# A graph-network layer on one core: a second tile of source columns in every fourth pair, built by VectorE, with narrower one-hots

## The reference, cut to what matters

```python
msg_in = jnp.concatenate([nodes[row], nodes[col], edge_features], axis=-1)
messages = relu(msg_in @ mW1 + mb1) @ mW2 + mb2
aggregated = jax.ops.segment_sum(messages, col, num_segments=nodes.shape[0])
upd_in = jnp.concatenate([nodes, aggregated], axis=-1)
x = _layernorm(x + relu(upd_in @ uW1 + ub1) @ uW2 + ub2)
```

## Time and profile before

| | us |
|---|---|
| median of 3 runs | 1884.84 (1877.70 to 1885.05) |
| the profiled execution | 1882.74 |
| its span, on which every time in the rows lies | 1880.9 |

### The profile page before, as it was taken

One profiled execution on the slowest core, in us unless ns is written; L12 is line 12 of the kernel. 1 busy time (PEld: TensorE's weight loads), 2 busy tenths in 40 slices (PEclk: granted clock), 3 DMA queues, 4 the chain that ended last, 5 costly groups with the idle time before them and its releaser, 6 DMA issues.

```text
span 1880.9 us, 44708 instructions
## 1 busy us (share of the span) xinstructions
PE 1466.1 (78%) x8940; PEld 1317.6 (70%) x8940; DVE 1374.8 (73%) x8194; ACT 1452.3 (77%) x12577; POOL 1383.9 (74%) x1478
## 2 busy tenths in 40 slices
PE   6777667787977778778977688777878887968778
PEld 6766667777766767667776677666767776867676
DVE  5746777787777777777777678778777777777773
ACT  4147878787888888888888878788787887887974
POOL 5677777777777777777777777777777777777772
PEclk9887778777787887887688877888786878787876
DMA  8555445544544544544544444454454454455441
GB/s 235 169 126 121 119 106 127 124 115 116 126 113 116 126 111 118 126 115 114 126 119 118 118 122 121 112 126 122 107 126 117 112 126 122 107 125 121 114 114 29
DMA packets 99674, 226.91 MB, mean 121 GB/s; under 512 B 45451, under 2 KB 61656, under 8 KB 86782
## 3 DMA queue, kind: packets, MB, share of 16 engines
q1 hardware_dynamic: 42532, 124.03, 26.3%
q0 software_dynamic: 46816, 94.40, 21.1%
q10 hardware_dynamic: 10046, 5.59, 1.2%
HBM read 214.24 MB, written 9.60 MB: 119 GB/s over the span
## 4 chain that ended last, share of the span: by engine, by line
POOL 71%; issue 23%; PE 3%; DMA 2%; DVE 1%; DVEq 0%; POOLq 0%; ACT 0%
POOL gath L798 68%; POOL hid L782 1%; DMA hid<-in_x_dram,idx_all 1%; DMA gath<-table_src,idx_all 1%; POOL raw_x L782 1%; PE ps_sum L934 1%; PE ps_pre L914 0%; DVEq L504 0%; DVE col_x L543 0%; DVE lhs L1275 0%; DVE hid L1304 0%; PE ps_pre L921 0%; PE ps_node L987 0%; PE ps_pre L981 0%; PE ps_pre L987 0%
## 5 line engine op out<-in xcount | busy, mean ns | idle before, releaser
L798 POOL DMA_INDIRECT gath<-table_src,idx_all x1415 | 1335.5, 944 | 431.2 <-issue 429.4
L520 ACT COPY col_x<-xz 64x1 f32 x11840 | 1137.3, 188 | 59.3 <-issue 55.0
L914 PE MATMUL ps_pre<-rhs,lhs 128*128 128x128 f32 x3226 | 576.2, 352 | 382.7 <-DVE lhs L1275 379.4
L914 PEld LDWEIGHTS ps_pre<-rhs,lhs 128*128 128x128 f32 x3226 | 536.9, 260 | 404.1 <-DVE lhs L1275 400.7
L543 DVE TENSOR_TENSOR col_x<-xz 64x2 int32 x6698 | 525.6, 148 | 135.9 <-issue 128.5
L934 PE MATMUL ps_sum<-onehot,hid 128*128 128x96 f32 x3322 | 471.9, 303 | 4.1 <-ACT rhs L1067 4.1
L934 PEld LDWEIGHTS ps_sum<-onehot,hid 128*128 128x128 f32 x3322 | 451.2, 218 | 25.6 <-issue 23.2
L1304 DVE TENSOR_TENSOR hid<-ps_pre,gath 128x1024 f32<-128x1024 f32 x202 | 246.7, 1221 | 288.1 <-DMA gath<-table_src,idx_all 269.8
L1105 ACT ACTIVATE hid<-hid 128x1024 f32<-128x1024 f32 x202 | 211.7, 1048 | 102.8 <-DVE hid L1304 99.0
L1275 DVE TENSOR_SCALAR_CACHE_REDUCE lhs<-lhs,place 96x1024 f32<-96x1024 int32 x208 | 262.1, 1260 | 15.7 <-DMA lhs<-in_dst_dram 15.7
L1268 DVE TENSOR_TENSOR onehot<-ps_iota,dst_rel 128x768 f32<-128x768 f32 (+1 forms) x209 | 196.7, 942 | 0.1
(11 more groups left out here) (136 smaller groups left out, 686.5 us busy)
## 6 DMA issues: line engine op xcount, KB each, us to landing
lhs<-in_dst_dram SPq DMA_DIRECT2D x99, 768.0 KB
lhs<-in_edgeT_dram SPq DMA_DIRECT2D x98, 256.0 KB
gath<-table_src,idx_all POOLq DMA_INDIRECT x1415
table_src<-gath SPq DMA_DIRECT2D x12, 512.0 KB, 7.5
xwin<-in_xT_dram SPq DMA_DIRECT2D x208, 24.0 KB
lhs<-in_dst_dram SPq DMA_DIRECT2D x10, 384.0 KB, 4.3
out_dram<-late_b ACTq DMA_DIRECT2D x48, 64.0 KB, 2.2
xz<-in_xT_dram ACTq DMA_DIRECT2D x4, 512.0 KB, 11.6
```

Of the source, the lines that this page charges most:

```text
L520: ins = copy(col_x[:, k, start + n + j:start + n + j + 1], col)
L798: pool.indirect_dma_start(gath[0:m, k, j * H:(j + 1) * H], None, table_src, src_by_tile(p, j, m)).then_inc(gathered[k], 16)
L914: mm = nc.tensor.matmul(to[0:m, j * H:(j + 1) * H], lhs[:, k, j * P:j * P + m], rhs[:, k, :], start=True, stop=not by_cols)
```

## The change

**In each fourth pair, a second tile by copied columns.** `EX_FIRST` is 15. For p = 15, 19, ..., 203 (48 pairs) the tile before the last, `EX_TILE`, is not gathered either. Its 128 columns are copied into the new tensor `col_e` (two buffers), all by DVE. The work is spread over four steps: in each step the function `extra` loads 16 registers and issues 8 two-column instructions, once in the middle of the step and once at its end. PE adds one matmul for the tile (L962 of the changed file).

**Early registers.** The two register loads of the first `col_x` batch move from behind the one-hots to ahead of `add_gathered`.

**Columns.** ACT copies 56 and DVE 72 (40 and 32), where they were 60 and 68.

**Narrow one-hots.** The first four tiles of a pair write only columns 0 to 47 of the window, the last four 20 to 75. The rest is zeroed once ahead of the loop (three memsets). The sums that DVE adds are 76 wide, not 96. PE's matmuls keep their width of 96. The check of the input is stricter to match: for the input here the destinations reach at most 33 nodes from the window's start in a pair's first half, and 27 to 65 in its second, so the same path is taken.

**Raw gathers.** POOL no longer waits between raw pairs.

```diff
-COL_ACT = 60
-COL_LOADS = (12, 16, 12, 12, 8)
+COL_ACT = 56
+COL_LOADS = (12, 16, 12, 8, 8)
 COL_DVE = 32
+EX_FIRST = 15
+EX_TILE = PT - 2
+EX_STEPS = 4
+EX_PART = P // EX_STEPS
...
+        def extra_of(p):
+            q = p + 2 + (EX_FIRST - p - 2) % SLOTS
+            return (q, EX_STEPS - (q - p - 1)) if has_extra(q) else None
...
-            return rows_of(p) if is_last(p) else PT - has_cols(p)
+            return rows_of(p) if is_last(p) else PT - has_cols(p) - has_extra(p)
...
             for r in range(RAW):
-                if r > 0:
-                    pool.wait_ge(raw_got[r - 1], 16 * PT)
...
+                    if extra:
+                        pe.wait_ge(cols_ext, ext_count(p))
+                        mm = nc.tensor.matmul(to[:, j * H:(j + 1) * H], col_e[:, p // SLOTS % 2, :], w_src[0:D, :], start=False, stop=True)
...
-                for first, t, m in parts(p):
-                    to = onehot[0:m, k, first * WIN:(first + t) * WIN].rearrange("p (t w) -> p t w", t=t)
+                for first, t, m, lo, hi in window_parts(p):
+                    to = onehot[0:m, k, first * WIN:(first + t) * WIN].rearrange("p (t w) -> p t w", t=t)[:, :, lo:hi]
...
+            def extra(p, half):
+                q, part = extra_of(p) or (None, None)
+                if q is not None:
+                    if q == EX_FIRST and part == 0 and half == 0:
+                        dve.wait_ge(cols_tabled, 8)
+                    start = part * EX_PART + half * EX_PART // 2
+                    held = load_regs(dve, q // SLOTS, start, EX_PART // 2, 2)
+                    join_batch(col_e[:, q // SLOTS % 2, :], start, held).then_inc(cols_ext, 1)
...
+                early = load_regs(dve, p + 1, DVE_FROM + COL_DVE, P - DVE_FROM - COL_DVE) if has_cols(p + 1) else None
                 if before and not is_raw(before[0]):
                     add_gathered(*before)
...
-                    done = join_batch(col_x[:, to, :], start, load_regs(dve, p + 1, start, P - start))
+                    done = join_batch(col_x[:, to, :], start, early)
                     done.then_inc(cols_dve, 1)
+                extra(p, 0)
...
                     join_batch(col_x[:, to, :], DVE_FROM, held).then_inc(cols_dve, 1)
+                extra(p, 1)
```

More of the change, by code:

```diff
@@ L49 @@
 WMAX = N - WIN
+WA = 48
+WB = 20
+W = 76
 NC = 256
@@ L106 @@
 TAB = (PAIRS + 2) // 2
+TABS = 3
 LAST_ROWS = TILES - 1
@@ L158, in gnn_kernel @@
         lane = sb("lane", [P, 1])
-        col_f = sb("col_f", [P, 2 * TAB])
-        col_tab = sb("col_tab", [P, 2, P], I32)
+        col_f = sb("col_f", [P, TABS * TAB])
+        col_tab = sb("col_tab", [P, TABS, P], I32)
         col_x = sb("col_x", [D, SLOTS, P])
+        col_e = sb("col_e", [D, 2, P])
         root = sb("root", [P, 1])
@@ L287, in gnn_kernel @@
         added = sem("added")
+        hot_zero = sem("hot_zero")
         centred = sem("centred")
@@ L375, in parts, with window_parts, width @@
             return ((0, TILES, P), (TILES, 1, TAIL)) if is_last(p) else ((0, PT, P),)
+        def window_parts(p):
+            if is_last(p):
+                return [(first, t, m, 0, WIN) for first, t, m in parts(p)]
+            return [(0, TILES, P, 0, WA), (TILES, TILES, P, WB, W)]
+        def width(p):
+            return WIN if is_last(p) else W
         def tiles_of(p):
@@ L480, in first_cols, with zero_from @@
             return has_cols(p) and col_before(p) is None
+        def zero_from(p):
+            return EX_TILE if p == EX_FIRST else COL_TILE if first_cols(p) else 0
         def zeroed_before(p):
-            return sum(first_cols(q) for q in range(p + 1))
+            return sum(zero_from(q) > 0 for q in range(p + 1))
         def two_of(p):
@@ L497, in gnn_kernel, with load_regs @@
         col_regs = count_up()
-        def load_regs(eng, p, start, count):
-            row, half = p % TAB, p // TAB
+        def load_regs(eng, p, start, count, part=None):
+            row, half = (p % TAB, p // TAB) if part is None else (p, part)
             regs = [eng.alloc_register(f"col{next(col_regs)}") for n in range(count)]
@@ L913, in pre @@
                     by_cols = has_cols(p) and (j == col_tile(p) or j == TILES and is_last(p))
+                    extra = has_extra(p) and j == EX_TILE
                     mm = nc.tensor.matmul(to[0:m, j * H:(j + 1) * H], lhs[:, k, j * P:j * P + m], rhs[:, k, :], start=True,
-                                          stop=not by_cols)
+                                          stop=not (by_cols or extra))
+                    if extra:
+                        pe.wait_ge(cols_ext, ext_count(p))
+                        mm = nc.tensor.matmul(to[:, j * H:(j + 1) * H], col_e[:, p // SLOTS % 2, :], w_src[0:D, :], start=False, stop=True)
                     if by_cols:
@@ L943, in step @@
                 if it * SLOTS + k == COL_MADE + 1:
-                    pe.wait_ge(cols_listed, 2)
-                    for half in range(2):
+                    pe.wait_ge(cols_listed, 4)
+                    for half in range(TABS):
                         ins = nc.tensor.transpose(ps_node[0:TAB, half * P:(half + 1) * P], col_f[:, half * TAB:(half + 1) * TAB], ident[:, :])
```

71 lines of the change are left out of this document (49 added, 22 removed).

## The result

| | before | changed |
|---|---|---|
| median, us | 1881.82 (1877.70 to 1885.05, 4 runs) | 2454.50 (2448.28 to 2456.01, 4 runs) |
| ratio, 95% interval | 1 | 1.3041 [1.3006, 1.3075] |
| the profiled execution, us | 1882.74 | 2453.39 |
| span, us | 1880.9 | 2451.6 |

A forecast was written before the change was run, and what follows sets the result against it. POOL's gathers were taken to bound the kernel, with DVE next; DVE's step would grow to 11.6 us. 1882.7 + 543 for 192 steps - 10 at the head = 2416 us, own range 2340 to 2500, overall range 2110 to 2530.

The forecast's parts named there:

- The bound and the next engine: POOL's gathers set the pace before, 8.74 us a pair; DVE, at 8.77 us a step, would be next.
- The price of a register: In DVE's register loads each register costs 0.063 us, with a base of 0.09 us a load.
- the walk: Changed DVE step followed from hid, taking the later of engine and sequencer each time; 2.45 us bare at its head.
- The queue of ten: About ten instructions can be queued ahead, seen on ACT and taken for DVE too.
- The first rival: DVE's queue takes all the sequencer gives, covering the load of 16; step 9.8 to 10.9 us, 2070 to 2280; chance 0.15.
- the second (overtaking): Hid and one-hots overtake the early loads on DVE; step about 9.5 us, time 2010 us; chance 0.08.
- the third: DVE's loads stay covered and POOL sets the end; step 8.43 us, about 1808 us; chance 0.07.
- The fourth: PE does not fit beside DVE's step in one step of four; 2480 to 2550 us; chance 0.07.
- Early works against the step: Loads ahead of hid lose their cover because DVE no longer waits there for a gather; 2.45 us bare.
- The sum: Profiled 1882.7 us plus 543 for DVE's steps minus 10 for the head gives 2416 us.
- 192 steps: DVE's steps 10 to 202 grow from 8.77 to 11.6 us each, +543 us.
- head, to hid of step 10: Raw gathers lose 22 us of waits where POOL leads, against three memsets of about 1 us each; -10 us taken.

The follow-up runs named there:

- e3: Kernel before plus two loads of 16 registers in each DVE step from 11 to 201, each followed by one two-column copy: 1958.82 us, ratio 1.040.
- e4: Kernel before plus 16 more two-column copies in each DVE step, from registers loaded anyway: 1878.50 us, ratio 0.999.
- e2: Changed kernel with the two register loads of the first batch back behind the one-hots, extra tile kept: 2199.75 us, ratio 1.168.
- e5: Kernel before with only the two register loads of the first batch moved ahead of hid: 1883.74 us, ratio 1.002.
- e6: Kernel before with only the waits between the raw pairs' gathers taken out: 1864.02 us, ratio 0.989.
- e9: Changed kernel with the extra tiles' address rows moved to partitions 56 to 103 of the table, from 3 to 50: 2470.76 us, ratio 1.314.

## Why the prediction was right, point by point

**The bound and the next engine** were read rightly: POOL leads before, and in the changed kernel DVE does (51% of the chain, in which POOL no longer stands). The sign was named too low in one place: POOL waits 646.5 us for hid, where some 500 was said.

**The price of a register** (0.063 us, from loads of 4 and 32) gave 1.10 us for the load of 16, measured 1.10 to 1.17 away from the slow stretches. That 32 more registers alone cost time and 16 more copies alone don't is shown by e3 and e4. That the copies are free in the full change is not, and the walk did not say so: it counted them at 1.2 us a step.

**The stalls by the walk** hold gap by gap. The queue of ten, taken over from ACT, is seen on DVE in every step. The first rival (a deep queue) falls with the load at 1406.4, the second (overtaking) with hid at 1403.98, the third (POOL sets the end at 1808) with everything. The fourth (PE joins in) asked for late PE; e2 shows hid waiting for nothing at a step of 10.48, and in the changed kernel DVE waits 20.0 us in all for PE's sums at L1393, so PE was not in the way.

**"Early works against the step"**: shown by e2, 255 us. By itself it costs nothing (e5): it needs a step in which DVE no longer waits for gathers.

**The sum**, 2415.7 before rounding, missed the profiled execution's 2453.4 by 37.7 us:

| term | forecast | measured | difference |
|---|---|---|---|
| 192 steps | 11.6 us each, +543 | 11.72, +567.8 | +24.8 |
| head, to hid of step 10 | -10 | 128.7 to 128.0, -0.7 | +9.3 |
| behind hid of step 202 | 0 | 69.2 to 72.8, +3.6 | +3.6 |

The term of the step came out near by luck in one part. The walk itself was right: it gave 11.2 us, and in steps 106 to 165 a step without a node block takes 11.23 to 11.26 us. A step with one takes 11.88, so the node block adds 0.16 on average where 0.1 was said. The 0.2 to 0.3 us that I added for slow issue are not there. In their place stands the crossing of partition 64, 0.82 us in each of 76 steps, 0.32 on average, of which no term spoke. Without it the forecast would have been too high by some 25 us instead of too low by 38.

The term of the head was wrong in its reason. POOL did begin its table gathers 20.6 us earlier (65.0 for 85.6 us), but the way to step 10 does not lead through POOL: it leads through DVE and PE, and there PE's first sum waits 4.7 us for the zeroing of the one-hots. I had put the three memsets at about 1 us each, which no row showed; they take 1.4 us together and cost more by their place. Alone on the kernel before, the raw edit is worth 18 us (e6), near the end of -22, and in the bundle 0.7 at step 10.

## What to carry to other kernels

Before work is given to an engine with idle time, its sequencer has to be counted too: register loads, waits and issue appear in no busy share, and here 7.1 to 8.0 us of a step of 11.7 were loads. In this kernel a load from memory into registers was free only under instructions that were already queued behind one another, so it belongs behind the longest ones, and never ahead of an instruction on which the step hangs unless the engine waits there for something else anyway. And of a bundle of edits, each is worth its own run: the two-line one here gains 1.1% by itself, and disappears in the bundle. Where a small piece of work stands counts as well: 1.4 us of memsets behind one of 9.45 us held up another engine by 4.3.

## What the runs showed of the hardware that was not expected

A register load takes about 0.23 us longer when its row lies on the other side of partition 64 than the row of the load before: 1.34 us for 1.10 with 16 registers, and e9 moved the effect by moving the rows. In this kernel it costs some 62 us, 0.82 us in 76 steps; a table for a program that alternates between two sets of rows is better kept on one side.
